# Turned row maxima of a two-layer softmax-attention kernel: from the row-score banks and VectorE to the column-score banks and ScalarE

## The reference

```python
q = relu(queries @ Wq_w.T + Wq_b); k = relu(keys @ Wk_w.T + Wk_b); v = relu(values @ Wv_w.T + Wv_b)
qh, kh, vh = _split_heads(q), _split_heads(k), _split_heads(v)      # 16 heads of 8
score = einsum('bhsd,bhtd->bhst', qh, kh) / sqrt(8)
attn = softmax(score, axis=-1)                                      # over the 512 keys
a = einsum('bhst,bhtd->bhsd', attn, vh)
```

## Time and profile before

| | |
|---|---|
| three runs | 692.82 to 697.38 us, median 696.42 |
| the profiled execution | 693.09 us, its span 691.0 us |
| mean granted TensorE clock over the span | 0.882 |
| PE, DVE, ACT, POOL busy | 534.5, 544.1, 421.8, 229.5 us |
| slots 0 to 31, from the first column item to the last copy of bank 7 | 72.8 to 423.4 us |
| what follows (the encoder layer) | 423.5 us to the end |

### The profile page before, as it was taken

One profiled execution on the slowest core, in us unless ns is written; L12 is line 12 of the kernel. 1 busy time (PEld: TensorE's weight loads), 2 busy tenths in 40 slices (PEclk: granted clock), 3 DMA queues, 4 the chain that ended last, 5 costly groups with the idle time before them and its releaser, 6 DMA issues.

```text
span 691.0 us, 9879 instructions
## 1 busy us (share of the span) xinstructions
PE 534.5 (77%) x3439; PEld 211.0 (31%) x3439; DVE 544.1 (79%) x899; ACT 421.8 (61%) x882; POOL 229.5 (33%) x360
## 2 busy tenths in 40 slices
PE   1874799999999889989899899576477765998620
PEld 1650122222222222222222113465356643443300
DVE  4969799999999989999899800488965555799996
ACT  2550588888888788887888863333445223474653
POOL 6001000000036330363203650085054600766761
PEclk9995699999999999999999955869777697999955
DMA  9732010112111122110211001100000000000102
GB/s 247 238 129 103 13 40 28 29 34 57 49 53 28 28 57 60 42 32 25 69 52 38 9 6 30 43 2 0 1 1 1 1 1 0 0 2 0 30 22 69
DMA packets 31286, 28.92 MB, mean 42 GB/s; under 512 B 6133, under 2 KB 23677, under 8 KB 31237
## 3 DMA queue, kind: packets, MB, share of 16 engines
q1 hardware_dynamic: 29204, 27.31, 13.5%
q10 hardware_dynamic: 2032, 0.98, 0.5%
HBM read 19.23 MB, written 8.65 MB: 40 GB/s over the span
## 4 chain that ended last, share of the span: by engine, by line
PE 43%; DVE 29%; POOL 11%; ACT 10%; issue 4%; DMA 2%; ACTq 0%; SPq 0%; DVEq 0%
PE ps L1249 14%; PE ps L1244 10%; DVE row_max L1417 10%; PE ps L1224 4%; PE ps L592 3%; ACT space L1352 2%; DVE space L871 2%; DVE st L241 2%; PE ps L508 2%; DVE SC L754 2%; DVE space L751 2%; ACT attended L1365 1%; POOL space L384 1%; POOL space L382 1%; PE ps L577 1%
## 5 line engine op out<-in xcount | busy, mean ns | idle before, releaser
L1417 DVE TENSOR_REDUCE row_max<-ps 128x2 f32<-128x1024 f32 x256 | 300.4, 1219 | 26.8 <-PE ps L1224 23.2
L1352 ACT ACTIVATE space<-ps 128x512 f32<-128x512 f32 x512 | 268.4, 605 | 66.4 <-PE ps L1244 66.4
L1244 PE MATMUL ps<-space 51*128 51x512 bf16 x512 | 158.1, 396 | 7.4 <-ACT space L1352 3.9
L1249 PE MATMUL ps<-space 128*32 128x512 f32 x1024 | 143.3, 633 | 0.7 <-ACT space L1352 0.7
L1224 PE MATMUL ps<-space 48*128 48x512 bf16 x512 | 130.0, 398 | 14.6 <-DVE row_max L1417 12.6
L1119 POOL CAST max_parts<-row_max 128x16 bf16<-128x16 f32 x32 | 6.3, 198 | 280.3 <-DVE row_max L1417 280.3
L1244 PEld LDWEIGHTS ps<-space 51*128 51x128 bf16 x512 | 38.6, 95 | 178.8 <-ACT space L1352 161.0
L592 PE MATMUL ps<-W,space 128*128 128x512 f32 x128 | 70.6, 634 | 0.0
L428 POOL TENSOR_TENSOR space<-PC,same_row 128x512 f32<-128x512 f32 x32 | 32.9, 1059 | 76.1 <-DVE PC L767 76.1
L709 ACT ACTIVATE space<-ps,weight 128x128 f32<-128x128 f32 x128 | 34.4, 384 | 20.8 <-PE ps L592 9.3
L1224 PEld LDWEIGHTS ps<-space 48*128 48x128 bf16 x512 | 29.1, 94 | 57.7 <-DVE row_max L1417 50.2
(11 more groups left out here) (192 smaller groups left out, 704.7 us busy)
## 6 DMA issues: line engine op xcount, KB each, us to landing
q_parts_dram<-space SPq DMA_DIRECT2D x2, 1536.0 KB, 5.4
space<-q_parts_dram SPq DMA_DIRECT2D x64, 48.0 KB
attended_dram<-attended SPq DMA_DIRECT2D x128, 18.0 KB
X<-in_L_attn_queries SPq DMA_DIRECT2D x8, 256.0 KB, 7.5
space<-in_L_ffn_w SPq DMA_DIRECT2D x2, 1024.0 KB, 6.0
space<-q_parts_dram SPq DMA_DIRECT2D x64, 32.0 KB
space<-attended_dram SPq DMA_DIRECT2D x16, 128.0 KB, 2.4
space<-inverses_dram SPq DMA_DIRECT2D x16, 128.0 KB
```

What stands on the lines that cost most here:

```text
L1244: pe.matmul(ps[:, col_bank(u), :], k_rows[rows_a, kappa // 4 % 2, tc * P:(tc + 1) * P], q_stack[rows_a, kappa % 4, b * S:(b + 1) * S], sta ...
L1249: mm = pe.matmul(ps[32 * m:32 * m + 32, PV, :], v_heads[:, tc, PAIR * (kappa // 4) + m % PAIR, :], probs[:, tc % 2, m, :], start=(tc == 0) ...
L1352: act.activation(probs[:, tc % 2, m, :], ps[:, col_bank(u), :], ACT.Exp, scale=1.0 / math.sqrt(DH)).then_inc(s_pr, 1)
L1417: dve.tensor_reduce(row_max[:, par].rearrange("p (a c) -> p a c", a=PAIR)[:, :, item], ring(n), AX.X, MAX).then_inc(s_free, 1)
```

## The change

The turn leaves the ring of row banks, which then holds eight items a slot. It takes a place in the sequence of the column banks instead: between C3 of block 1 and C0 of block 2, so that this sequence has 17 places a slot (`column_item` and `turn_item` number them). PE issues T in step 1 of the slot, behind C3, where it was at the end of step 0, ahead of V. Its copy to `max_turned` is an ACT instruction between `exps(kappa, 1)` and `exps(kappa, 2)`, and counts on `s_pr` as an exponential does; DVE's copy is gone. SP waits for that count ahead of `load_shift`. Before the loop the first turn stands behind four items of slot 1 instead of two. The counts in the waits of POOL and SP follow the new numbers. The diff, cut to its core:

```diff
+        col_bank = lambda v: 4 + v % 3
+        def column_item(kappa, tc, m):
+            return 1 + (TC * QB + 1) * kappa + QB * tc + m + (1 if tc > 1 and kappa + 1 < NQ else 0)
+        def turn_item(kappa):
+            return (TC * QB + 1) * (kappa - 1) + 1 + 2 * QB if kappa else 0
...
-                    sp.wait_ge(s_free, 17 + 9 * kappa + (3 if kappa + 2 < NQ else 1))
+                    sp.wait_ge(s_pr, turn_item(kappa + 1) + 1)
                     load_shift(kappa + 1)
...
-            def turn_max(n, par, waits, split):
-                pe.wait_ge(s_free, waits)
-                pe.wait_ge(s_split, split)
-
-                dst = ps[0:PARTS * QB * TC, 2 * (n % 2), 0:P // 2].bitcast(BF16)
-                pe.transpose(dst, max_parts[:, par].rearrange("p a r c -> p (a r c)"), ident16[:]).then_inc(s_full, 1)
+            def column_free(v):
+                if v >= 3:
+                    pe.wait_ge(s_pr, v - 2)
+
+            def turn_max(kappa):
+                v = turn_item(kappa)
+                pe.wait_ge(s_split, kappa + 1)
+                column_free(v)
+                dst = ps[0:PARTS * QB * TC, col_bank(v), 0:P // 2].bitcast(BF16)
+                pe.transpose(dst, max_parts[:, kappa % 2].rearrange("p a r c -> p (a r c)"), ident16[:]).then_inc(s_sc, 1)
...
-                score_columns(u + 3)
+                score_columns(kappa, tc, 3)
+                if tc == 1 and following:
+                    turn_max(kappa + 1)
...
-                if tc == 0 and following:
-                    last = n + 2 if ahead else n
-                    turn_max(last, (kappa + 1) % 2, last - 1, kappa + 2)
...
+            def copy_turned(kappa):
+                v = turn_item(kappa)
+                if kappa >= 2:
+                    act.wait_ge(s_shift, 32 * (kappa - 1))
+                act.wait_ge(s_sc, v + 1)
+                src = ps[0:PARTS * QB * TC, col_bank(v), 0:P // 2].bitcast(BF16)
+                act.copy(max_turned[:, kappa % 2, :], src).then_inc(s_pr, 1)
...
+            copy_turned(0)
             exps(0, 0)
             for kappa in range(NQ):
                 for tc in range(1, TC):
                     exps(kappa, tc)
+                    if tc == 1 and kappa + 1 < NQ:
+                        copy_turned(kappa + 1)
...
-            def copy_turned(n, par):
-                dve.wait_ge(s_full, n + 1)
-                src = ps[0:PARTS * QB * TC, 2 * (n % 2), 0:P // 2].bitcast(BF16)
-                dve.tensor_copy(max_turned[:, par, :], src).then_inc(s_free, 1)
```

More of the change, by code:

```diff
@@ L1216, in _, with score_rows @@
             project_half(1)
-            def score_rows(n, kappa, item, waits):
-                if waits is not None:
-                    pe.wait_ge(s_free, waits)
+            def score_rows(n, kappa, item):
+                if n >= 2:
+                    pe.wait_ge(s_free, n - 1)
                 for a in range(PAIR):
@@ L1226, in score_rows, with score_columns @@
                 mm.then_inc(s_full, 1)
-            def turn_max(n, par, waits, split):
-                pe.wait_ge(s_free, waits)
-                pe.wait_ge(s_split, split)
-                dst = ps[0:PARTS * QB * TC, 2 * (n % 2), 0:P // 2].bitcast(BF16)
-                pe.transpose(dst, max_parts[:, par].rearrange("p a r c -> p (a r c)"), ident16[:]).then_inc(s_full, 1)
-            def score_columns(u):
-                kappa, tc, m = u // (TC * QB), u // QB % TC, u % QB
-                if u % (TC * QB) == 0:
+            def column_free(v):
[7 more added lines that the diff above has]
+                pe.transpose(dst, max_parts[:, kappa % 2].rearrange("p a r c -> p (a r c)"), ident16[:]).then_inc(s_sc, 1)
+            def score_columns(kappa, tc, m):
+                if tc == TC:
+                    kappa, tc = kappa + 1, 0
+                if kappa == NQ:
+                    return
+                v = column_item(kappa, tc, m)
+                if tc == 0 and m == 0:
                     pe.wait_ge(s_shift, 32 * (kappa + 1))
-                if u >= 3:
-                    pe.wait_ge(s_pr, u - 2)
+                column_free(v)
                 rows_a = slice(HALF * (m % PAIR), HALF * (m % PAIR) + KALL)
                 b = m // PAIR
-                pe.matmul(ps[:, col_bank(u), :], k_rows[rows_a, kappa // 4 % 2, tc * P:(tc + 1) * P],
+                pe.matmul(ps[:, col_bank(v), :], k_rows[rows_a, kappa // 4 % 2, tc * P:(tc + 1) * P],
                           q_stack[rows_a, kappa % 4, b * S:(b + 1) * S], start=True, stop=True).then_inc(s_sc, 1)
@@ L1256, in _ @@
             pe.wait_ge(s_qe, B)
-            n = 0
             for item in range(8):
-                score_rows(n, 0, item, n - 1 if n >= 2 else None)
-                n += 1
+                score_rows(item, 0, item)
             pe.wait_ge(s_ql[1], 96)
             for item in range(8):
-                score_rows(n, 1, item, n - 1)
-                n += 1
-                if item == 1:
-                    turn_max(n, 0, n - 1, 1)
-                    n += 1
-            assert n == 17
-            pe.wait_ge(s_Wc, 2)
-            pe.wait_ge(s_csum, 1)
+                if item == 4:
+                    pe.wait_ge(s_Wc, 2)
+                    pe.wait_ge(s_csum, 1)
+                    turn_max(0)
+                score_rows(8 + item, 1, item)
             pe.wait_ge(s_vb, TC)
-            for u in range(QB - 1):
-                score_columns(u)
+            for m in range(QB - 1):
+                score_columns(0, 0, m)
             def step(kappa, tc):
-                n = 17 + 9 * kappa + 2 * tc + (1 if tc else 0)
-                u = QB * (TC * kappa + tc)
+                n = 8 * (kappa + 2) + 2 * tc
                 ahead, following = kappa + 2 < NQ, kappa + 1 < NQ
-                more = following or tc < TC - 1
-                score_columns(u + 3)
+                score_columns(kappa, tc, 3)
+                if tc == 1 and following:
+                    turn_max(kappa + 1)
                 if ahead:
@@ L1433, in _ @@
             for item in range(8):
-                reduce_rows(n, 1, item)
-                n += 1
-                if item == 1:
-                    copy_turned(n, 0)
-                    n += 1
+                reduce_rows(8 + item, 1, item)
             def slot(kappa, between):
-                n = 17 + 9 * kappa
                 for tc in range(TC):
```

49 lines of the change are left out of this document (20 added, 29 removed).

## The result

The kernel before has a median of 696.19 us (four runs, 692.82 to 697.38), the changed one 670.35 us (four runs, 668.69 to 670.79). The ratio is 0.9632, interval 0.9594 to 0.967: faster by 25.8 us, where 13.3 were forecast. The profiled executions are 693.09 and 670.79 us, their spans 691.0 and 669.0, so 22.0 us of the gain can be looked for in the traces. Of the other 3.8, 3.1 come from the profiled execution of before, which lay that much under the median of its kernel, 0.4 from that of after, which lay above its own, and 0.3 lie outside the spans. Ratios leave out runs that lie over 1.5% above the fastest of their kernel: beside the first four experiments five ordinary runs of the kernel before (695.85 to 697.97 us), since one run there took 685.14, and in start_filler two of its five, near 681.

The account below looks back on a forecast made before the run. It took a closed 2.39 us loop of C3, exponential, C2 and V to bound the plain step. Terms -12.2 - 2.8 + 3.0 - 1.3 = -13.3 us took 696.4 to 683 us, with eight in ten for 677 to 692.

Parts of the forecast that it names:

- What bounds the kernel: Attention slots: ACT and PE's order set the plain step, a closed loop of 2.39 us; a slot is 10.32 us.
- Part 1: Step 0: without T, V waits only for the copy of bank 7; 3.15 becomes 2.53 us, gain between 0 and 0.76.
- Part 2: Step 1: T and its copy enter, 0.15 for the copy, 0.06 for T; 2.39 becomes 2.60 us, at most 2.86.
- C2 has to wait for it: Step 1: the ACT copy of the turn isn't covered, C2 needs its bank and V follows C2; 0.15 us.
- rival B: Copy and T replace in step 1 what they free in step 0; slot 10.33 us, about 695 us; chance 0.14.
- Part 3: Slots where POOL is late: T one step later lets POOL's 12.37 us chain fit, DVE's excess stays; -2.8 us.
- Part 4: Slots 9, 17, 25: shift rows late behind SP's queue, 1.5 us stall each, 1.5 offset by the covered reciprocal; +3.0 us.
- Part 5: Beginning of the attention: table load moves behind the first turn's copy, done while rows are scored; -1.3 us, bounds -1.3 and 0.
- about the same at slot 30, whose T waits for POOL too: Slot 30: its wait for POOL saves about as much as each of two earlier slot groups, 0.95 us.
- the clock only as something that would show it wrong: Sign against the forecast: granted clock below 1.00 between 88 and 390 us.
- C: Rival: copy and T hidden altogether, slot 9.70 us, 18.3 saved instead of 12.2, 677 us; chance 0.12.
- D: Rival, slower: shift rows bound every slot; at 4.8 us issue to use, slot 10.74, about 704 us; chance 0.08.

Follow-up runs that it names:

- the first four experiments: Four of the follow-up runs, which four is not stated; beside them the kernel before had a median of 693.38 us.
- start_filler: Changed kernel with eight idle matmuls on PE among the last row items ahead of the loop: 669.08 us, ratio 0.9582.
- dve_copy: Changed kernel, turn in the column banks, but its copy done by DVE instead of ACT: 670.33 us, ratio 0.9635.
- copy_twice: Changed kernel with ACT's copy of the turned maxima made twice: 672.60 us, ratio 0.9658.
- r1_first: Changed kernel with R1 ahead of C1 in step 1 alone: 667.99 us, ratio 0.9598.
- changed_again: The changed kernel itself, unaltered, timed again in six runs: 668.05 us, ratio 0.9592.
- attended_halves: Changed kernel with SP issuing half of load_attended ahead of the slot and half behind, reciprocal and store_inverses moved later: 666.89 us, ratio 0.9577.
- table_early: Kernel before with a one-column exponential on ACT at the beginning of the attention, loading the table there: 693.77 us, ratio 1.0033.
- last_turn_step1: Kernel before with only the last turn (slot 31's) moved behind step 1's C3: 685.34 us, ratio 0.9897.
- last_split_late: Changed kernel with two idle multiplications on POOL ahead of the last splitting: 680.17 us, ratio 0.982.
- filler_last_turn: Kernel before with six idle matmuls on PE ahead of the last turn, which stays in place: 685.31 us, ratio 0.9897.
- r1_halves_tail: Changed kernel with R1 ahead of C1 in step 1, load_attended in halves, idle row matmuls in slots 30 and 31: 663.01 us, ratio 0.9519.

## Why the prediction was right, and where it was wrong

The direction and the main mechanism were right, the size was not: 670.35 us is below the whole range of 677 to 692. In the traces the sum is 8.7 us short (22.0 against 13.3), and 8.4 of them lie in slots 30 and 31. That the 29 slots ahead of them fit within 0.4 is in part luck, as told above.

**What bounds the kernel** held for the plain slots. Steps without the turn stayed at 2.39, and the closed loop of C3, exponential, C2 and V was the bound before and after.

**Part 1** (T leaves step 0): 2.55 where 2.53 was forecast, and V came right behind the copy of bank 7.

**Part 2** (T and copy in step 1): 2.61 where 2.60 was forecast, so the size was right, with some luck. Its reason was not: "C2 has to wait for it" is not what decides in the changed kernel. dve_copy changes nothing, copy_twice costs 0.08 for 0.25 us, and r1_first takes 0.08 away with the copy in place. C2 came late because C1 and R1 stood ahead of it behind C3's exponential. The forecast had this order only in rival B, as a delay for DVE, and not as a term of PE's own step. The forecast put 0.15 for the copy, near the 0.14 that r1_first leaves, and 0.06 for T, where PE's order costs 0.08.

**Part 3** (slots in which POOL is late): the five slots of the earlier trace rows that took 54.07 take 50.95 now, 1.2 over five plain ones, where the forecast left 1.5. POOL's chain is still 12.2 us, from the splitting at 209.08 to T at 221.32, and T waits 0.35 for it:

```profile
209.08 0.21 POOL max_parts L1137
...
221.32 0.24 PE ps L1248
```

**Part 4** (SP late): 3.8 instead of 4.5 in slots 9, 17 and 25, and in no other slot but for the 0.35 us at 95.50. The size varies between executions: in changed_again the three take 10.59, 10.47 and 11.00, 2.2 over. attended_halves shows that it was the queue, and that it could be had back.

**Part 5** (the table load): the load did move, from 73.51 to 66.73, and the first exponential came at 72.82 instead of 74.80, but the first copy of bank 7 only 0.4 earlier. The clock rose at about 83.6 instead of about 81.4, and the profiled executions of all kernels have that copy anywhere between 86.0 and 91.3. The part was within what the beginning varies by, and table_early shows none of it.

**The step that failed** is one clause of part 3, "about the same at slot 30, whose T waits for POOL too". It put 0.9 us for slots 30 and 31, by the length of the wait, and had no term for the clock; the runs show 9.3. The wait is 1.05 us, but it stands in a slot without row items, PE was busy for 1.84 of the 3 us from 395 to 398, and about 2 us later the clock fell to 1.2 GHz for 24 us. The last two slots took 27.9 us instead of 18.6. That was in the profile before: the clock row's two 5s at the end of the attention, the window of 0.50, and the intervals of 14.66 and 13.24 us between the last three copies of bank 7 for slots that have less to do than the others. The forecast listed the clock only as something that would show it wrong between 88 and 390, and stopped 9 us short of the place. The Trainium skill (TensorE: Matmul & The Clock Gate, Part 1: The HAM clock gate) says that the slow clock is the default and that PE's activity lifts it. last_turn_step1, last_split_late and filler_last_turn agree with it: the wait taken away, put back, and filled.

Rivals B, C and D did not come: no plain slot is at 10.33 or 9.70, and in slots 2 to 29 PE waits for shift rows only where SP's queue is long.

## What to carry to other kernels

Read the clock row over the whole span before the sum is made, and ask of each stretch at 1.2 GHz what PE waited for ahead of it: a wait of one microsecond in a thin stretch at the end of a loop cost nine here. Where an edit takes such a wait away, the stretch behind it is a term of its own. When two conditions hold an instruction, vary each alone (double one, reorder the other) before one is called the bound, and expect a saving elsewhere, like that of the banks here, to show in full only when the next bound (here SP's queue) is removed.

## What the runs showed of the hardware that was not expected

- The same turn with the same idle time ahead of it (0.34 and 0.35 us) was followed by a clock of 1.00 in one execution and 0.50 in another. Of the kernel before, two of the 13 runs beside the first four experiments took 685.14 and 689.44 us at a mean clock of 0.903 and 0.892, where the others had 0.871 to 0.882; that they kept the clock in the last slots is inferred from this, there is no trace of them. What decides it is open.
- The clock, at 1.00 until about 54 us in the trace of before and at 0.50 from 56 on, rose again at 81.4 us there, and between 77.8 (r1_halves_tail) and 86.8 us (start_filler) in the others; changed and changed_again, the same kernel, have 83.6 and 79.9. Eight more matmuls ahead of the loop did not make it earlier. This moves the whole attention by up to 5 us, and is open too.
